# Third layernorm and layer 3's first projections by groups beside the quantised feed-forward; binary weights made in layer 1's loop

## The reference, cut to what matters

```python
x = x + L0_conv(gn(x)); x = x + L1_conv(gn(x))        # super-token attention; 6-head attention with normalised weights
t = to_tokens(x)
t = t + L2_attn(ln(t))                                 # causal attention, 6 heads, 256 tokens an image
t = t + L2_ffn(ln(t))                                  # quantised feed-forward, below
t = t + L3_attn(ln(t))                                 # causal attention; this ln is the third layernorm
t = t + L3_ffn(ln(t))                                  # 4 experts, top 2

def binarize(W):                                       # 5 groups of rows, each: sign(w - mean of the group)
    for g in range(5): Wb[g*gs:(g+1)*gs] = sign(W[g*gs:(g+1)*gs] - W[g*gs:(g+1)*gs].mean())
def quantize(y):                                       # 5 groups of 3 images; the 16th image comes out zero
    for g in range(5): yq[3*g:3*g+3] = clip(y[3*g:3*g+3] * 128 / (abs(y[3*g:3*g+3]).max() + 1e-5), -128+1e-5, 128-1e-5)
L2_ffn = quantize(gelu(quantize(x @ binarize(W1).T + b1)) @ binarize(W2).T + b2)
```

## Time and profile before

| | us |
|---|---|
| median of 3 runs (871.05 to 877.22) | 876.08 |
| the profiled execution | 871.94 |
| its span, first to last instruction | 870.0 |

### The profile page before, as it was taken

One profiled execution on the slowest core, in us unless ns is written; L12 is line 12 of the kernel. 1 busy time (PEld: TensorE's weight loads), 2 busy tenths in 40 slices (PEclk: granted clock), 3 DMA queues, 4 the chain that ended last, 5 costly groups with the idle time before them and its releaser, 6 DMA issues.

```text
span 870.0 us, 17715 instructions
## 1 busy us (share of the span) xinstructions
PE 786.1 (90%) x5452; PEld 595.6 (68%) x5452; DVE 591.9 (68%) x1537; ACT 574.8 (66%) x1403; POOL 263.2 (30%) x516
## 2 busy tenths in 40 slices
PE   2988999999997979999997973699999978999997
PEld 1945877788776957777774672377777757777775
DVE  6145766767675347787873997378888834778775
ACT  3223878777775448888885823288888844787875
POOL 2702345665554441121211000112121210343334
PEclk9976999999999689999997986699999986999999
DMA  6000001101111123333331000332323212212320
GB/s 201 1 0 1 1 11 20 15 16 19 19 20 19 19 73 101 83 99 81 99 81 37 1 0 1 88 94 82 102 78 103 79 31 55 65 48 46 82 56 18
DMA packets 63270, 44.46 MB, mean 51 GB/s; under 512 B 34416, under 2 KB 55280, under 8 KB 63088
## 3 DMA queue, kind: packets, MB, share of 16 engines
q1 hardware_dynamic: 63216, 43.78, 19.8%
HBM read 12.24 MB, written 3.21 MB: 18 GB/s over the span
## 4 chain that ended last, share of the span: by engine, by line
PE 76%; DVE 10%; issue 6%; ACT 3%; POOL 3%; DMA 2%; SPq 1%; POOLq 0%; DVEq 0%
PE ps L1059 12%; PE ps L873 9%; PE ps L949 9%; PE ps L1205 7%; PE ps L1216 7%; PE ps L880 5%; PE ps L884 4%; PE ps L897 3%; PE ps L898 2%; PE ps L911 2%; PE ps L920 2%; PE ps L941 2%; PE ps L820 2%; PE ps L828 2%; POOL onn L387 1%
## 5 line engine op out<-in xcount | busy, mean ns | idle before, releaser
L549 ACT ACTIVATE ee<-ps,nmax 128x128 f32<-128x128 f32 (+1 forms) x584 | 207.4, 443 | 13.7 <-DVE nmax L1402 8.2
L1059 PE MATMUL ps<-w,ee 128*128 128x128 f32 x960 | 140.6, 275 | 3.3 <-ACT big L536 0.9
L1059 PEld LDWEIGHTS ps<-w,ee 128*128 128x128 f32 x960 | 111.0, 141 | 24.8 <-issue 9.3
L1402 DVE TENSOR_REDUCE nmax<-ps 128x2 f32<-128x256 f32 x200 | 101.7, 551 | 34.2 <-PE ps L884 33.4
L536 ACT ACTIVATE big<-ps 128x512 f32<-128x512 f32 (+1 forms) x192 | 97.2, 548 | 21.4 <-PE ps L1059 21.1
L1714 DVE TENSOR_TENSOR hhl<-ee,hhl 128x512 fp32r<-128x512 f32 x96 | 80.1, 840 | 31.2 <-ACT hhl L757 29.7
L873 PE MATMUL ps<-kh,big 128*128 128x256 f32 x384 | 95.5, 393 | 2.6 <-POOL big L327 1.6
L1399 DVE TENSOR_REDUCE nmax<-ps 128x4 f32<-128x1024 f32 x48 | 58.7, 1223 | 54.8 <-PE ps L873 54.8
L949 PE MATMUL ps<-big,vh 128*32 128x256 f32 (+1 forms) x1188 | 92.1, 353 | 0.0
L873 PEld LDWEIGHTS ps<-kh,big 128*128 128x128 f32 x384 | 72.3, 195 | 18.7 <-ACT ee L549 6.4
L464 POOL TENSOR_TENSOR xc<-big,xc 96x512 f32<-96x512 f32 x32 | 52.3, 1635 | 107.8 <-DVE big L1708 107.7
(11 more groups left out here) (255 smaller groups left out, 1359.1 us busy)
## 6 DMA issues: line engine op xcount, KB each, us to landing
qk<-hl SPq DMA_DIRECT2D x288, 96.0 KB, 3.1
big<-moe_gate SPq DMA_DIRECT2D x8, 768.0 KB, 6.9
w<-w_in SPq DMA_DIRECT2D x1, 1735.0 KB, 13.4
xc<-x_in SPq DMA_DIRECT2D x4, 384.0 KB, 5.9
l_mix<-on SPq DMA_DIRECT2D x32, 48.0 KB, 2.1
tok<-l_mix SPq DMA_DIRECT2D x16, 96.0 KB, 2.0
out<-xc SPq DMA_DIRECT2D x8, 192.0 KB, 2.1
w<-w_in SPq DMA_DIRECT2D x1, 998.0 KB, 9.7
```

Of the source, the lines that this page charges most:

```text
L549: last = nc.scalar.activation(ee[:, ke, hh, qc, 0:w], src, ACT.Exp, bias=nmax[:, kp, hh, qc:qc + 1])
L1059: last = nc.tensor.transpose(ps[:, 4 + hh, b * P:(b + 1) * P], ee[:, u, hh, qc, tc * P:(tc + 1) * P], ident)
L1402: last = V.tensor_reduce(out=nmax[:, kp, :, qc], in_=ps[:, 2 * kp:2 * kp + 2, qc * N:qc * N + scores_cols(l, qc)], axis=AX.X, op=ALU.max, ...
```

## The change

**Binary weights.** `weight_sums` runs on VectorE in layer 1 behind image 2's last unit; the two totals run on TensorE behind image 3's value projection, into spare columns of bank 7; `weight_centres` runs on VectorE in image 3 ahead of the value copy; `binary_weights(g)`, one pair of Sign passes, runs on ScalarE in the last unit of images 4 to 8. Layer 3's query weights are scaled at layer 1's start. TensorE does three of group 0's six first products (`first_layer(0, 0)`) before the last image's output is transposed back.

**Third layernorm.** Each f ends by raising `f2_stats`. Per group: ScalarE makes the root (Ln with epsilon as bias, Exp), GpSimd the shift (two small steps), then ScalarE scales the first half of the group's tiles and GpSimd the second half (group 4 has eight tiles), TensorE transposes into banks 3 and 4 (group 4: 4 and 5), ScalarE copies to `xn`. VectorE has no part in it. Image 0 is staged and projected behind group 0's copies, its low parts (`k0`) are VectorE's step before f4; image 1 follows behind group 2. The second product's second bank is 5 instead of 7 from group 1 on, since 7 now takes the projections. GpSimd follows a list of its own, F2_POOL; n is a group's layernorm, x an image's staging. The split of `w2hl` moves behind the staging of images 2 and 3.

```diff
-F2_DVE = [... "y3", "f2", "y4", "f3", "f4"]
+F2_DVE = [... "y3", "f2", "y4", "f3", "k0", "f4", "k1", "m0", "m1", "v0"]
+F2_POOL = ["a0", "a1", "a2", "a3", "y0", "a4", "y1", "y2", "n0", "y3", "n1", "x0", "y4", "n2", "x1", "n3", "n4"]
+        def y2_bank(g, b):
+            return 6 if b == 0 else 7 if g == 0 else 5
...
+                        elif step[0] == "n":
+                            lo, hi = ln3_tiles(g)
+                            pool.wait_ge(sg("norm_rs"), len(NORM) + g + 1)
+                            shift = st[:, 6, lo:hi]
+                            link(nc.gpsimd.tensor_tensor(shift, chmv[:, lo:hi, 0], st[:, 5, lo:hi], ALU.mult))
+                            nc.gpsimd.tensor_scalar(shift, shift, -1.0, None, ALU.mult).then_inc(sg("ln3_shift"), 1)
+                            for t in range((lo + hi) // 2, hi):
+                                last = nc.gpsimd.tensor_scalar(on[:, t, :], tok[:, t, :], chmv[:, t, 0:1], st[:, 5, t:t + 1], ALU.subtract, ALU.mult)
+                            last.then_inc(sg("ln3_normed_pool"), 1)
+                        else:
+                            pool.wait_ge(sg("l3_xn"), 2)
+                            stage(3, g, g)
...
                 if l == 3:
+                    nc.scalar.preload_act_table_set("natural_log_exp_and_others")
+                    for g in range(2):
+                        ln3_root(g)
+                        ln3_norm(g)
+                    ln3_channels(0)
                     queries(l, 0, 0)
+                    ln3_channels(1)
+                    ln3_root(2)
+                    ln3_norm(2)
+                    ln3_channels(2)
+                    ln3_root(3)
+                    ln3_norm(3)
                     queries(l, 1, 1)
+                    ln3_channels(3)
+                    ln3_root(4)
+                    ln3_norm(4)
                     exps(l, 0, 0, 0)
+                    ln3_channels(4)
...
+                    if l == 1 and u == 2 and 4 <= i < 4 + NG:
+                        binary_weights(i - 4)
...
+                if l == 3:
+                    ln3_transposes(0)
+                    pe.wait_ge(sg("l3_wq"), 1)
                     project_qk(l, 0, 0)
+                    ln3_transposes(1)
+                    ln3_transposes(2)
+                    parts_ready(l, 0)
+                    project_qk(l, 1, 1)
+                    ln3_transposes(3)
+                    keys_ready(l, 0, 0, 0)
+                    score_unit(l, 0, 0, 0, 0)
+                    pe.wait_ge(sg("l3_xn"), 7)
+                    score_unit(l, 0, 1, 1, 1)
+                    ln3_transposes(4)
+                    parts_ready(l, 1)
+                    project_v(l, 0, 0)
+                    pe.wait_ge(sg("f2_y2"), 2 * NG)
+                    mm(ps[0:C, 6, :], ident[:, 0:C], xn[:, B * N:(B + 2) * N], start=True, stop=True)
+                    pe.wait_ge(sg("l3_xn"), 2 * NG)
...
+                        if l == 1 and i == 3:
+                            pe.wait_ge(sg("f2_wsum"), 2)
+                            mm(ps[0:C, 7, 400:400 + NG], ones[0:C, 0:C], s64[0:C, 0, 0:NG], start=True, stop=True)
+                            mm(ps[:, 7, 408:408 + NG], ones[:, :], amax[:, 2, :], start=True, stop=True).then_inc(sg("f2_wtot"), 1)
...
+                if l == 2:
+                    pe.wait_ge(*upto(l, "max", 3 * B + 2))
+                    pe.wait_ge(*upto(l, "exp", 6 * B + 2))
+                    pe.wait_ge(sg("f2_w1z"), 1)
+                    pe.wait_ge(sg("f2_w1s"), NG)
+                    first_layer(0, 0)
                 if l > 1:
                     outputs_back(l, B - 1)
...
+                    if l == 1 and i == 2 and u == 2:
+                        weight_sums()
...
+                        if i == 3:
+                            weight_centres()
                         if i + 1 < B:
                             values(l, i + 1, npar)
```

More of the change, by code:

```diff
@@ L485, in norm_image @@
                                      scale=st[0:C, 5, i:i + 1]).then_inc(sg("gn0_xn" if name == "gn0" else "l1_xn"), 1)
[L487 to L498, removed]
+            def ln3_root(g):
+                lo, hi = ln3_tiles(g)
+                act.wait_ge(sg("f2_stats"), g + 1)
+                nc.scalar.activation(st[:, 3, lo:hi], chmv[:, lo:hi, 1], ACT.Ln, bias=eps[:, :]).then_inc(sg("norm_logs"), 1)
+                act.wait_ge(sg("norm_logs"), len(NORM) + g + 1)
+                nc.scalar.activation(st[:, 5, lo:hi], st[:, 3, lo:hi], ACT.Exp, scale=-0.5).then_inc(sg("norm_rs"), 1)
+            def ln3_norm(g):
+                lo, hi = ln3_tiles(g)
+                act.wait_ge(sg("ln3_shift"), g + 1)
+                for t in range(lo, (lo + hi) // 2):
+                    last = nc.scalar.activation(on[:, t, :], tok[:, t, :], ACT.Identity, bias=st[:, 6, t:t + 1], scale=st[:, 5, t:t + 1])
+                last.then_inc(sg("ln3_normed_act"), 1)
+            def ln3_channels(g):
+                for b in range(2):
+                    bank, t, n = ln3_place(g, b)
+                    act.wait_ge(sg("ln3_t_ps"), 2 * g + b + 1)
+                    nc.scalar.activation(xn[0:C, t * P:(t + n) * P], ps[0:C, bank, 0:n * P], ACT.Copy).then_inc(sg("l3_xn"), 1)
             nc.scalar.preload_act_table_set("natural_log_exp_and_others")
@@ L779, in group_squares @@
                 mm(ps[0:C, SUMS_AT[name], B + lo:B + hi], wb("avg3", C), st[0:C, 1, lo:hi], start=True, stop=True).then_inc(sg("gn_vg"), 1)
[L781 to L790, removed]
+            def ln3_transposes(g):
+                pe.wait_ge(sg("ln3_normed_act"), g + 1)
+                pe.wait_ge(sg("ln3_normed_pool"), g + 1)
+                for b in range(2):
+                    bank, t0, n = ln3_place(g, b)
+                    if g >= 1:
+                        pe.wait_ge(sg("l3_xn"), 2 * g - 1 + b if g < NG - 1 else 2 * g)
+                    for t in range(n):
+                        last = nc.tensor.transpose(ps[0:C, bank, t * P:(t + 1) * P], on[:, t0 + t, :], ident)
+                    last.then_inc(sg("ln3_t_ps"), 1)
             pe.wait_ge(sg("w128_loaded"), 16)
@@ L990, in project_mixed @@
                 last.then_inc(sg("l1_y_ps"), 1)
+            def first_layer(g, b):
+                pe.wait_ge(sg("causal_xn"), 3 * g + 3)
+                for j in range(NJ):
+                    a = g * GT + b * (GT // 2)
+                    pe.wait_ge(sg("f2_y1"), g * 6 + (b * NJ + j + 1))
+                    mm(ps[:, b * NJ + j, 0:GT // 2], wa("f2_w1")[:, j * P:(j + 1) * P], xn[:, a:a + GT // 2],
+                       start=True, stop=True).then_inc(sg("f2_y1_ps"), 1)
             def normed_back(g):
@@ L1649, in _ @@
                                             apply_absolute_value=True).then_inc(sg("f2_amax1"), 1)
+                        elif what == "k":
+                            keys(3, g, g)
+                        elif what == "m":
+                            maxima(3, g, g)
+                        elif what == "v":
+                            values(3, g, g)
                         else:
```

182 lines of the change are left out of this document (74 added, 108 removed).

## The result

The changed kernel takes 877.75 us (median of 20 runs, 873.92 to 881.03), the kernel before 872.63 us beside it (20 runs, 870.58 to 881.16). The ratio is 1.0041, 95% interval 1.0023 to 1.0060: slower by 0.4%, where 855 was forecast. The profiled execution took 878.5 us with a span of 876.6.

A forecast was written before the change was run, and what follows sets the result against it. TensorE fills three quarters of the chain, so gains must come from two stretches where it stands still. -6.5 + 0.7 - 13.5 = -19.3: 852.6 from the profiled 871.94, 856.8 from the median; forecast 855, range 846 to 866.

The forecast's parts named there:

- Both stretches: Stretches where TensorE stands still: the start of the quantised feed-forward, and the passage from it into layer 3 (25.9 us).
- Part A: Binary weights in layer 1, early first products: a1 earlier by 6.5 us at the feed-forward's start, bounds -1.5 and -7.3.
- The cost in layer 1: Layer 1, TensorE-bound: the moved sums, totals, centres and Signs add 0.7 us, bounds 0 and +4.8.
- Rival 4: Layer 1: Sign outside the set of Exp and Ln, two table loads in each of five images, 12.8 us back: 868; chance 0.02.
- Part B: Third layernorm by groups, passage into layer 3: first score 11.6 us earlier, with a later wait gone -13.5; bounds -9.3 to -15.5.
- under 3.4, as f4 never waited for y4's: Bound on the unseen real length of GpSimd's reduction: up to 3 us more at n1 or n2.
- the split of the second weights: GpSimd's queue in layer 3's loop: the 3.7 us split moved behind two stages, hidden since the next is due an image later.
- Rival 2: f4 on VectorE held behind k0 by a late first projection; within 1% of before, 865.5 and more; chance 0.07.
- Rival 3: GpSimd's tiles in groups 2 to 4: gain gone at 2.65 us a tile, over 1% slower from 3.5: 883; chance 0.03.
- Rival 1: Both parts work but shorter: clock falls at the feed-forward's start or reductions stretch the layernorm's ping-pong; 864; chance 0.19.
- ten serial tiles at 0.72: GpSimd's layernorm tiles in n2, n3 and n4, in series on the path into layer 3, costing 7.2 us.
- the second stack: Second image's stacked keys in layer 3: land at 543.5, before the loop's first score, so the 1.90 us wait before 564.40 goes.

The follow-up runs named there:

- experiment 1: Changed kernel with GpSimd's share of the third layernorm moved to VectorE and ScalarE's roots taken earlier; 851.24 us, ratio 0.9748 to the kernel before.
- part A alone: Kernel before plus binary weights in layer 1 and the early first products, third layernorm as it was; 868.56 us, ratio 0.9943.
- experiment 4: Kernel before plus one unused 128x6 multiplication on GpSimd between the reductions of y3 and y4; 880.99 us, ratio 1.0084.
- experiment 2: Changed kernel with GpSimd's list reordered so all reductions precede the layernorm's arithmetic; 865.22 us, ratio 0.9903 to the kernel before.

## Why the prediction was wrong

**What bounds the kernel: right.** Both stretches moved, and most of the miss stands in them. The profiled execution took 878.5 where 852.6 was forecast for it, 25.9 us more. The loop's first score came 24.6 us later than forecast (565.02 instead of 546.2 less 5.8). The passage to the experts, which the prediction does not name, added 2.9 at its lower clock. Against that, the start of the loop gave back 2.8 us instead of the 1.9 forecast, and the experts 0.7.

**Part A: right, the size within the bounds.** -6.5 was forecast for the stretch; it is 21.1 - 15.7 = -5.4 in the changed kernel, because the clock fell after all, and -7.2 in experiment 1, where it held: both lie between the bounds of -1.5 and -7.3. The cost in layer 1 was forecast at +0.7: layer 2's last product starts 0.8 us later in the changed kernel, 0.2 with part A alone, 1.6 in experiment 1. Most of that is not layer 1's: a small product that it runs once an image (L967 before) starts for the first time at 114.85 before, at 115.35 in the changed kernel and at 115.95 in experiment 1. From there to its sixteenth and last time it is 171.12 us before, 171.26 in the changed kernel and 171.29 in part A alone and in experiment 1. So the work that was moved costs layer 1 some 0.15 us, nearer the lower bound than the 0.7. Forecast net -5.8, measured -5.0 alone.

**Rival 4, the table switch: rightly excluded.** The changed kernel has four table loads as before. A pair of Signs takes ScalarE 0.6 us (`146.36 0.37 ACT L612`, `146.61 0.35 ACT L616`) where 0.5 was forecast, and the images that hold them (146.4 to 195.5) are as long as before: from the third to the eighth row of the small product named above it is 61.54 us before (139.78 to 201.32) and 61.55 after (140.41 to 201.96).

**Part B: the step that failed is GpSimd's queue.** The text put n1 at "0.5 for two small steps (0.24 the larger) and three tiles at 0.72" behind y3's reduction, and ended it at 522.7. It took each operation on GpSimd at its own row's duration and the passage from one to the next as nothing. The durations were right: three tiles took 2.05 us, 0.68 each, four 2.71, and the reduction's row 0.35. The passages were 5.9 to 7.1 us, and four of them stand one behind the other on the path. The bound "under 3.4, as f4 never waited for y4's" was a bound for a reduction behind a reduction, and the change puts it behind arithmetic. (The terms listed for one group also add up to 5.4, not 5.3; that moves the forecast by 0.2 us and explains nothing.)

The trace of before held the price. This is GpSimd in it, at the feed-forward's start and behind the first staging:

```profile
464.19 0.51 POOL L349 TENSOR_TENSOR onn<-onn,lnr 128x192 f32<-128x192 f32 x1
480.40 0.38 POOL L453 PARTITION_ALL_REDUCE amax<-amax  x1 [15.71 <-DVE amax L1630]
...
543.25 1.14 POOL L403 CAST w2hl<-w 128x1152 fp32r<-128x1152 f32 x1
551.21 2.60 POOL L405 TENSOR_TENSOR w2hl<-w,w2hl 128x1152 fp32r<-128x1152 f32 x1 [6.82 <-issue]
```

The arithmetic at 551.21 is the first after the reductions, and stands 6.82 us behind the row ahead of it with nothing to wait for but that row. The prediction priced this very step (3.7 us for the split of the second weights, moved and hidden) by its busy time and passed over the bracket. Not every bracket under "issue" is such a price: the 17.63 in front of the staging at 542.56 is a wait for ScalarE's last copy, which ends at 542.38 (`541.79 0.59 ACT L498`), 0.18 ahead of it. The other change of kind, at 480.40, lies in a wait of 15.71 us and can't be seen. Experiment 4 is what the trace could have suggested: the price is there in the kernel before as soon as the two kinds alternate.

The Trainium skill ("GPSIMD Engine Reference", section "2.1 Instruction dispatch") says that the first call into a freshly loaded GpSimd kernel pays a load of code of about 6 us that has no instruction of its own in a profile. The trace agrees in the size and the look of it (5.8 to 7.8 us under "issue"); whether code is loaded in that time, no run here shows.

**Rival 2 was the nearest, dismissed for a reason that did not hold.** It named the place, f4 on VectorE behind k0, and its cause, "a stall of x0 behind n1", and set it aside because n1 would end 1.1 us before x0 could start. n1's tiles ended at 534.28 instead of 522.7 less A's 5.8, x0 was staged at 534.26, and VectorE stood 9.15 us in front of k0 (`537.45 0.69 DVE L1467`). **Rival 3** looked for the loss on the right engine, but in the length of a tile; the tiles were as forecast. **Rival 1** bounded the reductions at 3 us.

**The rest of part B was right, once GpSimd is out of it.** With the same tiles on VectorE (325 ns each in the median, as the 322 of the earlier trace rows) the step from part A alone (868.56) to experiment 1 (851.24) is -17.3 us. The forecast was -13.5 with ten serial tiles at 0.72. With VectorE's tiles ScalarE's half of a group ends last, and TensorE's transposes wait for it (`529.85 0.86 PE L830`, idle 2.23 for ScalarE); in groups 2 to 4 it takes 1.17, 1.17 and 1.53 us, 3.9 instead of 7.2, so the same sum gives 3.3 more, -16.8. The times agree with the grouping, the early projection and the second stack as the sum had them; no run tests these one by one. Both parts together are -22.6 of 873.82, where -19.3 was forecast.

**Chances and range.** The range ended at 866 and the time was 877.75: the range left out any cost that shows in no row of its own. The result, +0.4%, lies within 1% of before, which had 0.11, most of it from rival 2. Slower by over 1% had 0.04, 0.03 of it from a tile's length.

## What to carry to other kernels

Before work is put on an engine between operations of another kind, look in the trace for every place where that engine goes over from one kind to the other, and read the bracket behind the first row after it: a time under "issue" at which all that the instruction needs was there is a price per change, and it counts once for each alternation in the new order. On GpSimd reductions over partitions and arithmetic (`tensor_tensor`, `tensor_scalar`) should come in blocks, with copies, and fills between reductions, wherever they fit. Where they must alternate on a path that decides the time, move the arithmetic to another engine even if that engine is the busier one: here VectorE took 16 tiles, with the roots on ScalarE earlier, and the kernel gained some 26 us against the version that spared it.

## What the runs showed of the hardware

- GpSimd's change from reductions to arithmetic took 6.7 to 7.8 us (7.76 at the split of the second weights in experiment 4), the change back 5.8 to 6.0, wherever no longer wait covered it; copies (0.25 us) and fills (0.17 us) took no such time behind a reduction.
- The change runs while the next instruction waits for its data. In experiment 1 the first reduction of the feed-forward comes 8.54 us after arithmetic, and starts as VectorE's maximum (472.14 + 2.55 = 474.69) is there:

```profile
465.78 0.51 POOL L363 TENSOR_TENSOR onn<-onn,lnr 128x192 f32<-128x192 f32 x1
474.83 0.38 POOL L466 PARTITION_ALL_REDUCE amax<-amax  x1 [8.54 <-DVE amax L1679]
```

  So a change of kind is free where the engine stands idle for longer than that ahead of it. In the changed kernel n0 shows the same: its data was there at 511.11, 2.2 us after the reduction's end, and it started 6.83 after that end, not 6.8 after its data.
- TensorE's granted clock behind layer 2's last product differed between kernels with the same code there: 1.00 throughout in experiments 1 and 2, down to 0.50 from 470 to 472 in the changed kernel. In the passage to the experts it did so too, and 2.9 us went with it.
